# Two waits for GpSimd in a two-layer graph attention kernel: the low part of the next x behind the ELU's minimum, the low part of x1 behind both first normalisations

## The reference

```
# layer 0: six heads of 64, masked softmax over the neighbours
q, k, v = x @ Wq + bq, x @ Wk + bk, x @ Wv + bv
ctx = softmax(q k^T / 8 + bias(adj)) v
x1 = layernorm(x + ctx @ Wf + bf)
# layer 1: twelve heads of 32, additive attention, then ELU and a gate
h = x1 @ W;  th = tanh(h)
attn = leaky_relu(th . w_src + (th . w_dst)^T, 0.2), masked, softmax
f = elu(attn @ h + b)
gate = sigmoid(x1 @ H_w^T + H_b)
out = layernorm(x1 + gate * f + (1 - gate) * x1)
```

## Time and profile before

| what | value |
|---|---|
| median of three runs | 1142.79 us (1141.11 to 1144.12) |
| the profiled execution | 1140.15 us |
| its span, first to last instruction | 1138.4 us |
| TensorE, matmuls, busy | 1003.7 us, 88% of the span |
| VectorE busy | 1018.4 us, 89% |
| ScalarE busy | 983.8 us, 86% |
| GpSimd busy | 795.1 us, 70% |
| chain of waits that ended last | VectorE 39%, issue 25%, TensorE 13%, ScalarE 7%, GpSimd 4% |

### The profile page before, as it was taken

The page is one execution under the profiler, slowest core; times in us unless marked ns, Lnnn a source line. Parts: engine busy times, 40 slices in busy tenths (PEclk is TensorE's granted clock), DMA queues, the critical chain, the costliest instruction groups (busy, mean ns, idle before and its releaser), DMA issues.

```text
span 1138.4 us, 32966 instructions
## 1 busy us (share of the span) xinstructions
PE 1003.7 (88%) x10570; PEld 826.3 (73%) x10570; DVE 1018.4 (89%) x1969; ACT 983.8 (86%) x2315; POOL 795.1 (70%) x653
## 2 busy tenths in 40 slices
PE   5799999999999999999999999999999999998540
PEld 5778877778787777787777778777777888775320
DVE  6878998999999999999999999999999999999762
ACT  4559998999999999999999999999999999998663
POOL 2146877777787777777777777787777677776664
PEclk9899999999999999999999999999999999999875
DMA  5025653555554445555544555554445555445543
GB/s 199 16 76 119 132 130 93 124 120 144 132 135 124 116 118 122 122 145 130 128 116 106 124 119 145 131 129 126 108 117 123 133 142 128 121 118 104 100 98 83
DMA packets 315187, 136.50 MB, mean 120 GB/s; under 512 B 268944, under 2 KB 310160, under 8 KB 315152
## 3 DMA queue, kind: packets, MB, share of 16 engines
q1 hardware_dynamic: 315152, 136.06, 49.5%
HBM read 30.56 MB, written 12.58 MB: 38 GB/s over the span
## 4 chain that ended last, share of the span: by engine, by line
DVE 39%; issue 25%; PE 13%; ACT 7%; POOL 4%; DMA 2%; DVEq 2%; SPq 2%; ACTq 1%; POOLq 0%
PE gen L502 9%; ACT p_hi L847 3%; DVE z L1189 3%; DVE z_max L1196 3%; DVE sd L1020 3%; DVE stats L1164 2%; DVE y L1160 2%; DMA p1t_lo<-p_lo 2%; DVE k_lo L994 2%; DVE p L1116 2%; DVE stats L1233 2%; DVE q_lo L991 2%; POOL rstd L1393 2%; DVE p_off L1125 2%; DVE x L1184 2%
## 5 line engine op out<-in xcount | busy, mean ns | idle before, releaser
L1405 POOL TENSOR_TENSOR p_lo<-z,p_hi 128x1536 f16<-128x1536 f32 x64 | 199.8, 3122 | 59.0 <-ACT p_hi L847 59.0
L839 ACT ACTIVATE z<-z,z_off 128x128 f32<-128x128 f32 x768 | 231.8, 400 | 0.0
L1361 POOL TENSOR_TENSOR prod<-th,w_sd_rows 128x768 f32<-128x768 f32 x64 | 117.8, 1841 | 47.5 <-ACT th L760 47.5
L1410 POOL TENSOR_TENSOR f<-f,x_kept 128x384 f32<-128x384 f32 x64 | 64.3, 1004 | 92.0 <-DVE f L1228 92.0
L812 ACT ACTIVATE p<-p,p_off 128x128 f32<-128x128 f32 x384 | 118.8, 394 | 1.1 <-DVE p_off L1125 1.0
L666 PEld LDWEIGHTS gen<-h_part,p1t_hi 128*128 128x128 f16 x1536 | 61.5, 96 | 79.8 <-issue 33.5
L666 PE MATMUL gen<-h_part,p1t_hi 128*128 128x33 f16 x1536 | 67.4, 179 | 58.8 <-DMA p1t_lo<-p_lo 46.1
L502 PE MATMUL gen<-W_hi,x1t 128*128 128x384 f16 x384 | 105.8, 331 | 9.1 <-DMA x1t<-x_part 4.9
L1189 DVE SCALAR_TENSOR_TENSOR z<-zp,z 128x1536 f32<-128x1536 f32 x64 | 112.0, 1749 | 1.5 <-ACT z L821 1.3
L1196 DVE TENSOR_REDUCE z_max<-z 128x12 f32<-128x1536 f32 x64 | 111.5, 1742 | 0.0
L502 PE MATMUL gen<-Hw_hi,x1t 128*128 128x384 f16 x384 | 105.2, 329 | 0.0
(11 more groups left out here) (171 smaller groups left out, 3907.1 us busy)
## 6 DMA issues: line engine op xcount, KB each, us to landing
xt_raw<-x_t SPq DMA_DIRECT2D x32, 384.0 KB, 3.4
x_raw<-x SPq DMA_DIRECT2D x32, 384.0 KB, 3.1
x_held<-x SPq DMA_DIRECT2D x64, 192.0 KB, 2.4
x_kept<-x_held SPq DMA_DIRECT2D x64, 192.0 KB, 2.2
out<-out_tile SPq DMA_DIRECT2D x64, 192.0 KB, 1.9
mask_kept<-mask SPq DMA_DIRECT2D x32, 64.0 KB, 1.8
mask<-mask_kept SPq DMA_DIRECT2D x32, 64.0 KB, 1.9
adj<-adj SPq DMA_DIRECT2D x32, 32.0 KB, 1.8
```

The lines of the kernel that those rows point to most:

```text
L839: last = act.activation(z[:, g, N * h:N * (h + 1)], z[:, g, N * h:N * (h + 1)], ACT.Exp, bias=z_off[:, g, h:h + 1])
L1361: pool.tensor_tensor(prod[:, g, :].rearrange("p (s d) -> p s d", s=2), th[:, g:g + 1, :].to_broadcast([128, 2, D]), rows["w_sd"][:, :].rea ...
L1405: pool.tensor_tensor(p1_lo[:, g, :], z[:, g, :], p1_hi[:, g, :], ALU.subtract).then_inc(w1_lo[g].sem, 1)
L1410: pool.tensor_tensor(f[:, g, :], f[:, g, :], x1_kept[:, g, :], ALU.subtract).then_inc(f_diff[g].sem, 1)
```

## The change

Two steps of GpSimd get one more wait each. `next_x_low` now also waits for `f_min` of graph 0, which VectorE signals at the end of `features_negative(0)` of the same turn. `first_low(g)`, for both graphs, now also waits for `x1_ready` of graph 1, which VectorE signals at the end of `norm0(1)` of the same turn. No instruction is added, removed or moved on any engine; what the two steps compute and where they stand in GpSimd's list is as before, and so are the lists of the other engines. From here on the line numbers of GpSimd's steps behind the first new wait are one or two higher.

```diff
                 def next_x_low():
+                    pool.wait_ge(f_min[0].sem, prev(f_min[0]))
                     pool.wait_ge(xt_hi_made.sem, now(xt_hi_made))
                     pool.tensor_tensor(xt_lo[:, :, :].rearrange("p c n -> p (c n)"),
                                        xt_raw[:, :, :].rearrange("p c n -> p (c n)"),
...
                 def first_low(g):
+                    pool.wait_ge(x1_ready[1].sem, prev(x1_ready[1]))
                     pool.wait_ge(x1_high[g].sem, now(x1_high[g]))
                     pool.wait_ge(x1_turned[g].sem, prev(x1_turned[g]))
                     pool.tensor_tensor(x1_part[:, g, 1, :], x1[:, g, :], x1_part[:, g, 0, :], ALU.subtract)\
```

## The result

The changed kernel takes 1110.79 us (median of four runs, 1107.61 to 1112.98) against 1141.95 us before (four runs, 1140.85 to 1144.12). The ratio is 0.9723 with a 95% interval of 0.9692 to 0.9753: 31 us less. Forecast were 1106 us and a range of 1095 to 1124. The profiled execution took 1112.05 us, 28.1 less than the one before, and its span is 1110.3 us.

What follows compares the result with a forecast made beforehand. VectorE was taken to bound the turn, TensorE and ScalarE 0.4 to 1.0 us behind. 17 x 1.53 + 7 x 0.97 = 32.8, plus 1.2, is 34 us off 1140.15: 1106 us, range 1095 to 1124.

Steps and rivals of the forecast that it cites:

- f_neg(0) stands behind xt_lo for 1.51 us: VectorE's minimum for graph 0 takes 1.87 us beside GpSimd's xt_lo; with the wait it takes 0.36.
- Of that, 1.25 us reach the turn: From f_neg(0) to z_leak(0): 1.25 us less in all 25 turns, taken between 1.03 and 1.44.
- three routes: Ways to z_leak(0): ScalarE could come forward by 1.03 us, TensorE by 1.23, VectorE by 1.51.
- The wait on GpSimd costs nothing: xt_lo ends 0.7 us later, but GpSimd's 1.36 us of idle time ahead of v_part covers that.
- The second part: x_part waits for norm0(1): 0.56 us gained in 17 long turns, 0.28 us lost through rstd in all 24.
- A turn that was short before: One of 7 turns of 32.51 us with norm0(1) at 0.47 us; the 17 long ones take 33.07.
- The rival of the new stall: elu(0) on VectorE is held 0.39 us behind GpSimd's v_part; 0.13 us a turn lost, 1109 us; chance 0.06.
- The sum: 1.53 us less in 17 long turns, 0.97 in 7 short ones: 32.8 us, with 1.2 more 34 us.
- TensorE did not take over at once: Rival: TensorE is next late, only its own wait of 0.52 us comes off; 1124 us; chance 0.13.
- p_lo never held f_neg(0): Slower rival: f_neg(0) arrives while GpSimd's p_lo runs and is held, at worst 3.34 us; 1170 us; chance 0.05.
- the sum was not used whole: Rival that all is used: 1.44 us a turn and rstd costs nothing; 45.5 us less, 1095 us; chance 0.12.

Runs made afterwards that it cites:

- e1: Against the kernel before, only the first wait: GpSimd's low part of the next x waits for f_neg(0); 1110.65 us, ratio 0.9716.
- e5: Changed kernel plus deviation1 ahead of value_part3(1) on GpSimd and the transpose of p_lo(0) ahead of the xt_raw load on SyncE; 1091.89 us.
- e2: Against the kernel before, only the second wait: the low part of x1 waits for norm0(1); 1140.68 us, ratio 0.9982.
- e4: Against the kernel before, no wait added; f_neg written in the form with two tensor inputs, both in SBUF; 1152.39 us, ratio 1.0092.

## Why the prediction was right, step by step

- **f_neg(0) stands behind xt_lo for 1.51 us.** Right: 0.36 us in all turns, and e1, with this wait alone, has the whole gain.
- **Of that, 1.25 us reach the turn.** The size was right, but in part by luck. Over the 24 turns the stretch from f_neg(0) to the end of z_leak(0) fell from 11.58 to 10.31 us in the mean, by 1.27. In the turn above it fell by 11.60 - 10.17 = 1.43 us; in the next it is 602.02 - 591.54 = 10.48 us, 1.12 less. The two differ by TensorE: ahead of the second one its attend1(0) waited 0.83 us for the transpose of p_lo, ahead of the first one 0.47, and the sums for VectorE's f_rcp came later. In e5, where this wait is gone, the stretch is 10.15 to 10.22 us in all 24 turns, 1.41 less than before. So none of the three routes that I had named set the 1.25. ScalarE's 1.03 and TensorE's 1.23 were both passed, and what held the mean down was a wait for a DMA that I had not counted.
- **The wait on GpSimd costs nothing.** Right: the gap ahead of v_part took it up, with nothing left over, and behind v_part GpSimd still waits 0.57 us for VectorE's f. The start of xt_lo came 0.23 us after the end of f_neg(0), not 0.15.
- **The second part, +0.56 and -0.28.** The mechanism was right and the cost was sized too small. A turn that was short before should lose 0.28 us and loses 0.36 in e2; one that was long should gain 0.56 - 0.28 = 0.28 and gains 0.17. rstd went from 0.35 to 0.63 us, the 0.28 of the forecast, but x_part started 0.25 us after norm0(1)'s end (570.57 to 570.82), not 0.15, so that mix and with it the statistics came later too. From the start of norm0(1) to that of rstd it is 4.70 us, where the short turn has 4.61: 0.28 + 0.09 = 0.37 us. The 0.15 us had been read from a longer pass that signals GpSimd.
- **The rival of the new stall came true beside the forecast.** elu(0), at 563.08, runs into v_part of 562.41 and takes 0.63 us where it took 0.55. It ends 563.71 - 563.30 = 0.41 us behind v_part, the same 0.41 as in e4. I had put the hold at 0.39 us, with the tail of the one-source form, as if the pass were put off by all of it; the pass is 0.55 us long by itself, so only 0.08 us of it shows. These do reach the stretch: f_neg(0) gave back 1.51 us, and 1.51 - 0.08 = 1.43 is what the stretch lost in this turn.
- **The sum.** Forecast for the 24 turns were 32.8 us; the traces give 789.6 - 759.2 = 30.4. The second part, 0.11 us too high in 17 turns and 0.08 in 7, accounts for about that. In the profiled execution the start was 4.0 us later and the end 1.7 us shorter, so 28.1 us remain of 34. By medians it is 31.2.
- **The other rivals** did not occur: TensorE did not take over at once, p_lo never held f_neg(0) (it ends at 559.87, and f_neg(0) starts at 560.02), and the sum was not used whole either, since TensorE kept a gap of 0.45 us for z_leak and one for the transpose. But the argument against using it whole, that a turn of 31.07 us would leave TensorE no gap, did not hold: the turn of e5 is 31.03 us, and in the one at 549.91 TensorE is busy for 30.41 us and still waits for z_leak.

## What to carry to other kernels

The same instruction on the same shape with two lengths can be a stall that no idle column shows; look at what the neighbouring engine runs at that moment, and subtract the ends. A wait that makes one engine step aside is free only as far as that engine has idle time right behind it, and everything queued behind it moves as well, perhaps into the next pass of the same kind: here half a microsecond gained at one place was paid back at another until a second exchange in the list. And read what two kinds of turn in one trace differ in before changing anything; they are an experiment that has already been made.

## What the runs showed of the hardware that I had not expected

- A VectorE pass that reads two tensors from SBUF is held by GpSimd's subtraction like the fast form with one source: 2.03 us against 0.56. Its tail behind GpSimd's end is 0.41 us; that of the one-source 128x384 form is 0.22 us.
- The length of a pass gives no protection. rstd, 128x2 values and 0.17 us alone, takes 0.62 to 0.65 us in the changed kernel, and ends 0.03 us behind GpSimd's instruction.
- The DMA transpose of p_lo, which takes 3.6 to 3.8 us to land in e5, takes 4.3 to 4.8 in the changed kernel when the 384 KB load of xt_raw is issued just ahead of it.
